# Counting edges in 39 steps, one of them 17 destinations wide, in a two-layer graph kernel

## The chip, the cores and the metric

The kernel runs on one core of a Trainium2 chip. The metric is device time in microseconds (us) of one execution. The kernel before takes 991.92 us, the median of 3 runs (991.07 to 992.71).

## The reference, cut to what matters

There are 625 nodes with 1024 features and 20000 edges (source, destination, one of 8 types), sorted by destination. A graph attention layer comes first, a relational layer with a gate second; each adds its input and is normalized over the features.

```python
def _L0_gnn_ref(x, W, a, src, dst):
    h = x @ W
    al = h @ a_l
    ar = h @ a_r
    e = jnp.exp(-jax.nn.leaky_relu(al[src] + ar[dst], negative_slope=NEG_SLOPE))
    rowsum = jax.ops.segment_sum(e, src, num_segments=N)
    h_prime = jax.ops.segment_sum(e[:, None] * h[dst], src, num_segments=N)
    h_prime = h_prime / (rowsum[:, None] + EPS)
    return jax.nn.elu(h_prime)

    # second layer
    for r in range(weight.shape[0]):
        mask = (edge_type == r).astype(x.dtype)
        sums = jax.ops.segment_sum(msgs * mask[:, None], dst, num_segments=n)
        cnt = jax.ops.segment_sum(mask, dst, num_segments=n)
        mean = sums / jnp.maximum(cnt, 1.0)[:, None]
        out = out + mean @ weight[r]
```

Both layers need the edges only as counts: how many edges of type r go from source s to destination d. The first layer multiplies these counts, summed over r, into its attention matrix; the second multiplies each type's counts with x.

## The kernel before

The five engines run programs written out by hand, tied by semaphores. Four stages follow each other on TensorE: h = x @ W in two halves of 512 columns (0 to 51 us); counting the edges, with the rest of that product, the sums of counts and the first attention products between the counting steps (51 to 148 us); the end of the attention, ELU, normalization and transposes (148 to about 190 us); and the second layer, a long row of fp32 products in three parts each (high by high, low by high, high by low).

Counting works as follows. The edges lie in 158 tiles of 128, one edge per partition. For each edge, `oh_s` holds a one-hot of its source within a block of 128 nodes (128 columns). VectorE builds a second one-hot for a *step* w (a window of `WIN` = 16 destinations): 640 columns, one for each pair of (source block, type) code and destination in the window, 40 codes by 16 destinations. That is `table` plus 16w compared with the edge's `key` (L968). TensorE multiplies the transposed first by the second in two matmuls of 320 columns into two banks of the accumulation memory (L1341). Both engines take tiles in *passes* of `BODY` = 5 tiles. The number of passes of a step depends on the data: setup code turns the smallest and largest destination of each tile and the edges of each step's window (`win_edge`) into a first tile and a number of passes, and each engine loads them from `lohi_row` at the head of the step (L345). A step counts ceil(tiles / 5) passes.

There are 40 steps for 640 destinations, though there are 625 nodes: the fortieth serves destination 624 alone. A step is, on TensorE: two small matmuls that clear the banks (L1356, waiting until ScalarE has copied the last step that used them), the passes, a small matmul that closes (L1359). On ScalarE: `copy_window`, one copy of 128x640 from the banks to `Cst` (L595). On VectorE: five one-hots for each pass.

Two buffers hold the one-hots, `hot` for even steps and a part of `w_raw` for odd ones, five slots each; semaphores `built` and `counted` guard each slot. So VectorE builds the next step's while TensorE multiplies this step's, but two passes of one step share one buffer. From step 12 on the steps alternate between two pairs of banks, 2/3 and 5/6 (`window_bank`, which counts from the last step back); before that all use 5/6.

The other work of this stage is tied to step numbers. After step 8(j+1) and the three behind it, TensorE sums a block of 128 destinations over the types (L1293) and turns it (L1300). `att_mult(3)` (VectorE, L948) and `att_high(3)` (ScalarE, L627) come after step 38, `att_low(3)` (VectorE, L953) after step 39. Behind the last step TensorE starts `att_h(1, 0, ...)` (L1306 to L1308) into banks 2 and 3, waiting for the copies of all steps but the last, then L1293 for the last block, waiting for the copies of all.

Of the kernel before, what the change touches and what calls it, by code (L numbers as in the profile page):

```python
# [5 lines left out]
def gat_rgcn_kernel(nc, dst_cols, src_cols, type_cols, dst_units, xT, x, weights, a, bias, b_gate, counts_dram, out):  # L6
# [4 lines left out]
    i32 = mybir.dt.int32  # L11
# [24 lines left out]
    WIN = P // R  # L36
    WINDOWS = NP // WIN
    PER = P // WIN
    CODES = NT * R
    SPLIT = NP // 2  # L40
    NE = N + N % 2
    NCOL = [(0, 320), (320, NE - 320)]
# [6 lines left out]
    GB = 3  # L49
    SUMS = 2 * KT  # L50

    def rows(t):
# [6 lines left out]
    with ctx:  # L59
# [33 lines left out]
        key = sb("key", [P, ALL_TILES], f32)  # L93
        table = sb("table", [P, NP], f16)
        ident = ident_r[:, :].bitcast(f32)
# [3 lines left out]
        with ExitStack() as first:  # L99
            xT_raw = sb("xT_raw", [P, KT, N], f32, first)  # L100
            iota_i = sb("iota_i", [P, NP], i32, first)
            h_raw = sb("h_raw", [P, NT, H2], f32, first)
# [56 lines left out]

        hots_in = [hot[:, :], w_ring[:, :, :].rearrange("p b n -> p (b n)").bitcast(bf16)[:, 0:BODY * NP]]  # L160

        def one_hot(w, s, c0=0, c=NP):
            return hots_in[w % 2][:, s * NP + c0:s * NP + c0 + c]

        edge_rows = table[0:2, :].bitcast(f32)

# [185 lines left out]
        def _(sp):  # L352
# [13 lines left out]
            def flush(j):  # L366
                sp.wait_ge(window_copied, PER * (j + 1) + 1)
                for m in range(NT):
                    sp.dma_start(C_dram[:, m, :, j * P:(j + 1) * P].rearrange("r p n -> p r n"),
                                 Cst[j % 2][:, m, :, :].bitcast(f32)).then_inc(flushed[j], 16)  # L370
# [95 lines left out]
        def _(pool):  # L466
            pool.iota(iota_i[:, :], pattern=[[1, CODES], [P // 2, WIN]], base=0, channel_multiplier=0).then_inc(pool_consts, 1)
            pool.iota(part_col[:, :], pattern=[[0, 1]], base=0, channel_multiplier=1,
# [76 lines left out]
        def _(act):  # L545
# [43 lines left out]
            def copy_window(w):  # L589
                j, v = divmod(w, PER)  # L590
                act.wait_ge(window_counted, w + 1)
                if v == 0 and j >= 2:
                    act.wait_ge(flushed[j - 2], 16 * NT)
                    act.wait_ge(turned, 2 * (j - 1))
                nc.scalar.copy(Cst[j % 2][:, :, :, v * WIN:(v + 1) * WIN].rearrange("p m r d -> p (m r) d")  # L595
                               .rearrange("p (b q) d -> p b q d", b=2),
                               ps[:, window_bank(w) * H2:(window_bank(w) + 2) * H2]
                               .rearrange("p (b n) -> p b n", b=2)[:, :, 0:SPLIT]
                               .rearrange("p b (q d) -> p b q d", d=WIN)).then_inc(window_copied, 1)
# [205 lines left out]
        def _(dve):  # L805
# [21 lines left out]
            step(v.memset(dots[:, :], 0.0))  # L827
            dve.wait_ge(pool_consts, 6)
            v.tensor_scalar(table[:, :], iota_i[:, :], 1.0 / (P // 2), None, ALU.mult)
            v.tensor_scalar(ident_r[:, :], iota_s[:, :], part_col[:, :], None, ALU.is_equal)  # L830
            v.tensor_scalar(win_edge[:, 0:1], part_col[:, :], float(WIN), None, ALU.mult)
            step(v.tensor_scalar(win_edge[:, 1:2], part_col[:, :], float(WIN), float(WIN - 1), ALU.mult, ALU.add))
            def split_low(n, k):
# [128 lines left out]
            def hots(w):  # L962
                turn = turns[w % 2]
                n = dve.snap(turn, min_val=1, max_val=WINDOWS * ALL_TILES)
                tile = dve.snap(tile_at, min_val=0, max_val=ALL_TILES - BODY)
                for s in range(BODY):
                    dve.wait_ge(counted[w % 2][s], n)
                    v.tensor_scalar(one_hot(w, s), table[:, :], float(WIN * w),  # L968
                                    key[:, ds(tile + s, 1)], ALU.add, ALU.is_equal).then_inc(built[w % 2][s], 1)
                dve.reg_add(turn, turn, 1)  # L970
                dve.reg_add(tile_at, tile_at, BODY)
# [244 lines left out]
        def _(pe):  # L1216
# [69 lines left out]
            def sum_counts(j, part):  # L1286
                m0, m1 = turn_blocks(part)
                pe.wait_ge(window_copied, PER * (j + 1) + 1)
                if turn_bank(j, part) == 4:
                    pe.wait_ge(turned_read, 2 * j + part)  # L1290
                o = bank(turn_bank(j, part), c=(m1 - m0) * P).rearrange("p (m n) -> p m n", n=P)
                for r in range(R):
                    last = mm(o, ident_r[:, :], Cst[j % 2][:, m0:m1, r, :], start=r == 0, stop=r == R - 1)  # L1293
                last.then_inc(summed, 1)
# [39 lines left out]
            def counts(w):  # L1334
# [3 lines left out]
                for s in range(BODY):  # L1338
                    pe.wait_ge(built[w % 2][s], n)
                    for c in range(2):  # L1340
                        last = mm(bank(window_bank(w) + c, c=SPLIT), oh_s[:, ds(edge + s * P, P)],  # L1341
                                  one_hot(w, s, c * SPLIT, SPLIT),
                                  start=False, stop=False, skip_group_check=True)
# [248 lines left out]
```

## Time and profile before

| | |
|---|---|
| median of 3 runs | 991.92 us (991.07 to 992.71) |
| the profiled execution | 990.91 us, its span 989.1 us |
| TensorE matmul busy | 977.2 us, 99% |
| VectorE, ScalarE, GpSimd busy | 392.9, 281.7, 254.2 us |
| mean granted TensorE clock | 0.998 |
| one-hots built (L968) | 210, 381 ns each |
| counting matmuls (L1341) | 420, 299 ns each, 210 on each buffer |

The profile shows one execution. The span is the time between its first and last instruction. Matmuls overlap one another, so the time that one costs is the distance of starts, not its duration. Idle time of an engine costs something only where TensorE, which is busy all along, waits for it.

### The profile page before, as it was taken

The numbers are of one execution on the slowest core, as the hardware profiler recorded it, in microseconds if no ns is written. First come the engines' busy times: TensorE is split into PE (matmuls) and PEld (weight loads), VectorE is DVE, ScalarE is ACT, GpSimd is POOL, SyncE is SP. The second block draws the span as 40 slices with busy tenths as digits, with TensorE's granted clock in tenths as the row PEclk, the third lists the DMA queues.
The fourth block names the chain that finished last, engine by engine and source line by source line (L and its number), as shares of the span: only waits on it lengthen the run. The fifth ranks groups of instructions, "written<-read, shape, count | busy, mean of one in ns | idle before, by whom it ended". The sixth has DMA issues, their size and how long they took to land.

```text
span 989.1 us, 14598 instructions
## 1 busy us (share of the span) xinstructions
PE 977.2 (99%) x5138; PEld 820.9 (83%) x5138; DVE 392.9 (40%) x749; ACT 281.7 (28%) x486; POOL 254.2 (26%) x196
## 2 busy tenths in 40 slices
PE   9999999999999999999999999999999999999997
PEld 7866778778898888888888988988988988888886
DVE  7998883712222331430530430331232232202277
ACT  4324554741122122121221221222222212212432
POOL 0000002084322323213223122142141231326730
PEclk9999999999999999999999999999999999999999
DMA  7204657067210411411411321231141051212402
GB/s 266 64 2 129 186 182 228 11 227 201 77 42 22 163 44 32 151 43 43 140 53 43 116 77 43 95 99 42 30 153 41 12 172 36 71 52 66 139 1 104
DMA packets 69005, 91.41 MB, mean 92 GB/s; under 512 B 9396, under 2 KB 35475, under 8 KB 68838
## 3 DMA queue, kind: packets, MB, share of 16 engines
q1 hardware_dynamic: 68818, 90.57, 29.1%
q8 instruction: 23, 0.38, 0.2%
q10 hardware_dynamic: 148, 0.32, 0.1%
q14 instruction: 16, 0.13, 0.0%
HBM read 75.19 MB, written 15.69 MB: 92 GB/s over the span
## 4 chain that ended last, share of the span: by engine, by line
PE 96%; DVE 2%; ACT 1%; issue 1%; POOL 0%; DVEq 0%; ACTq 0%
PE ps L1225 21%; PE ps L1227 21%; PE ps L1226 21%; PE ps L1493 9%; PE ps L1492 9%; PE ps L1341 6%; PE ps L1293 1%; PE ps L1548 1%; PE ps L1547 1%; PE ps L1546 1%; PE ps L1306 1%; PE ps L1307 1%; PE ps L1308 1%; PE ps L1481 0%; PE ps L1513 0%
## 5 line engine op out<-in xcount | busy, mean ns | idle before, releaser
L481 POOL TENSOR_TENSOR w_lo<-w_raw,w_hi 128x512 fp32r<-128x512 f32 x168 | 217.4, 1299 | 693.4 <-ACT w_hi L557 693.2
L557 ACT CAST w_hi<-w_raw 128x512 fp32r<-128x512 f32 x183 | 114.0, 625 | 463.8 <-PE ps L1227 397.6
L1225 PE MATMUL ps<-w_hi,M_hi 128*128 128x512 f32 (+1 forms) x550 | 215.6, 392 | 0.1
L1227 PE MATMUL ps<-w_lo,M_hi 128*128 128x512 f32 (+1 forms) x550 | 214.3, 390 | 0.0
L1226 PE MATMUL ps<-w_hi,M_lo 128*128 128x512 f32 (+1 forms) x550 | 214.2, 389 | 0.0
L1090 DVE SCALAR_TENSOR_TENSOR u<-ps,scale,u 128x512 f32<-128x512 f32 (+1 forms) x90 | 66.4, 745 | 315.0 <-PE ps L1227 315.0
L1492 PE MATMUL ps<-C_hi,x_hi 128*128 128x320 f32 (+3 forms) x640 | 184.5, 306 | 0.0
L1493 PE MATMUL ps<-C_hi,x_lo 128*128 128x320 f32 (+3 forms) x640 | 184.3, 306 | 0.0
L1225 PE MATMUL ps<-w_hi,M 128*128 128x512 f32 (+1 forms) x360 | 140.3, 390 | 0.0
L1227 PE MATMUL ps<-w_lo,M 128*128 128x512 f32 (+1 forms) x360 | 140.2, 390 | 0.0
L1226 PE MATMUL ps<-w_hi,M 128*128 128x512 f32 (+1 forms) x360 | 140.2, 389 | 0.0
L1492 PEld LDWEIGHTS ps<-C_hi,x_hi 128*128 128x128 f32 (+1 forms) x640 | 120.7, 189 | 0.9
L1225 PEld LDWEIGHTS ps<-w_hi,M_hi 128*128 128x128 f32 (+1 forms) x550 | 101.9, 185 | 23.3 <-issue 0.6
L1493 PEld LDWEIGHTS ps<-C_hi,x_lo 128*128 128x128 f32 (+1 forms) x640 | 120.9, 189 | 0.3
L1227 PEld LDWEIGHTS ps<-w_lo,M_hi 128*128 128x128 f32 (+1 forms) x550 | 101.8, 185 | 23.1
L1226 PEld LDWEIGHTS ps<-w_hi,M_lo 128*128 128x128 f32 (+1 forms) x550 | 101.9, 185 | 22.2
L1227 PEld LDWEIGHTS ps<-w_lo,M 128*128 128x128 f32 (+1 forms) x360 | 66.7, 185 | 15.0
L1226 PEld LDWEIGHTS ps<-w_hi,M 128*128 128x128 f32 (+1 forms) x360 | 66.7, 185 | 14.7
L1225 PEld LDWEIGHTS ps<-w_hi,M 128*128 128x128 f32 (+1 forms) x360 | 66.7, 185 | 14.6
L1095 DVE TENSOR_REDUCE col_sum<-C_hi 128x640 f32<-128x3200 f32 x8 | 47.9, 5987 | 42.8 <-DMA C_hi<-C_dram 42.8
L1111 DVE TENSOR_TENSOR M_lo<-ps,M_hi 128x320 fp32r<-128x320 f32 x64 | 31.0, 484 | 53.3 <-ACT M_hi L729 53.3
L1111 DVE TENSOR_TENSOR M<-ps,M 128x320 fp32r<-128x320 f32 x64 | 31.0, 484 | 53.3 <-ACT M L729 53.3
(189 smaller groups left out, 829.2 us busy)
## 6 DMA issues: line engine op xcount, KB each, us to landing
w_raw<-weights SPq DMA_DIRECT2D x184, 256.0 KB, 2.9
C_dram<-Cst SPq DMA_DIRECT2D x25, 512.0 KB, 6.1
C_hi<-C_dram SPq DMA_DIRECT2D x8, 1600.0 KB, 7.0
z<-b_gate SPq DMA_DIRECT2D x5, 512.0 KB, 9.6
u<-bias SPq DMA_DIRECT2D x5, 512.0 KB, 7.8
xT_raw<-xT SPq DMA_DIRECT2D x7, 312.5 KB, 6.7
u<-x SPq DMA_DIRECT2D x4, 512.0 KB, 4.8
last_raw<-weights SPq DMA_DIRECT2D x8, 256.0 KB, 5.5
```

Of the source, the lines that this page charges most:

```text
L481: pool.tensor_tensor(w_lo[k % RING][:, :], w_raw[k % RING][:, :], w_hi[k % RING][:, :].bitcast(f32), ALU.subtract).then_inc(w_lo_done, 1)
L557: nc.scalar.copy(w_hi[k % RING][:, :], w_raw[k % RING][:, :]).then_inc(w_hi_done, 1)
L1090: v.scalar_tensor_tensor(u[r, t, half * H2:(half + 1) * H2], bank(t, rows(t)), scale[odd][r, t:t + 1], u[r, t, half * H2:(half + 1) * H2], ...
L1095: v.tensor_reduce(col_sum[:, :], C_hi[:, :, :].bitcast(f32).rearrange("p m n -> p n m"), X, ALU.add)\
L1111: v.tensor_tensor(M_lo[1 - odd][:, e // 2, c0:c0 + cn], bank(5 + (e + 1) % GB, c=cn), M_hi[1 - odd][:, e // 2, c0:c0 + cn].bitcast(f32), A ...
L1225: mm(o, lhs_hi[:, k, c], w_hi[k % RING][:, :], start=opens, stop=False)
L1226: mm(o, lhs_lo[:, k, c], w_hi[k % RING][:, :], start=False, stop=False)
L1227: last = mm(o, lhs_hi[:, k, c], w_lo[k % RING][:, :], start=False, stop=closes_)
L1293: last = mm(o, ident_r[:, :], Cst[j % 2][:, m0:m1, r, :], start=r == 0, stop=r == R - 1)
L1341: last = mm(bank(window_bank(w) + c, c=SPLIT), oh_s[:, ds(edge + s * P, P)], one_hot(w, s, c * SPLIT, SPLIT), start=False, stop=False, ski ...
L1492: mm(o, x1_hi[r, m, f], C_hi[r, m, c0:c0 + cn], start=m == 0, stop=False)
L1493: last = mm(o, x1_lo[r, m, f], C_hi[r, m, c0:c0 + cn], start=False, stop=m == NT - 1)
```

## The change

There are 39 steps. Step 37 (`WIDE`) takes 17 destinations, 592 to 608, and step 38 takes 609 to 624; `win_at(w)` gives a step's first destination. The wide step's one-hots have `HOT` = 680 columns, and its second matmul 360. Its `copy_window` has an ACT copy of 128x40 ahead of the usual one, for the seventeenth destination. `win_edge` is built with two more VectorE instructions and `table` is 40 columns longer, for which there is one more iota on GpSimd. Since `window_bank` counts back from the last step, the bank pairs of all steps from 12 on change places: step 12 is now on 5/6 and 13 is the first on 2/3. The hunks that are left out replace `PER * (j + 1) + 1` by its minimum with 40 in two waits (`flush`, `sum_counts`).

```diff
-    WINDOWS = NP // WIN
+    WINDOWS = N // WIN
+    WIDE = WINDOWS - 2
     PER = P // WIN
     CODES = NT * R
     SPLIT = NP // 2
+    HOT = NP + CODES
+    assert N == WINDOWS * WIN + 1 and WIDE % 2 == 1
...
+    def win_at(w):
+        return WIN * w + (w > WIDE)
+
+    def cols(w):
+        return HOT if w == WIDE else NP
...
-            pool.iota(iota_i[:, :], pattern=[[1, CODES], [P // 2, WIN]], base=0, channel_multiplier=0).then_inc(pool_consts, 1)
+            pool.iota(iota_i[:, 0:NP], pattern=[[1, CODES], [P // 2, WIN]], base=0, channel_multiplier=0).then_inc(pool_consts, 1)
+            pool.iota(iota_i[:, NP:HOT], pattern=[[1, CODES]], base=WIN * (P // 2), channel_multiplier=0).then_inc(pool_consts, 1)
...
+                d0 = win_at(w) - j * P
+                if w == WIDE:
+                    nc.scalar.copy(Cst[j % 2][:, :, :, d0 + WIN].rearrange("p m r -> p (m r)"),
+                                   bank(window_bank(w) + 1, c0=SPLIT, c=CODES))
+                nc.scalar.copy(Cst[j % 2][:, :, :, d0:d0 + WIN].rearrange("p m r d -> p (m r) d")
...
-            v.tensor_scalar(win_edge[:, 0:1], part_col[:, :], float(WIN), None, ALU.mult)
-            step(v.tensor_scalar(win_edge[:, 1:2], part_col[:, :], float(WIN), float(WIN - 1), ALU.mult, ALU.add))
+            v.tensor_scalar(win_edge[:, 0:1], part_col[:, :], float(WIDE), None, ALU.is_gt)
+            step(v.tensor_scalar(win_edge[:, 1:2], part_col[:, :], float(WIDE), float(WIN - 1), ALU.is_ge, ALU.add))
+            for c in range(2):
+                step(v.scalar_tensor_tensor(win_edge[:, c:c + 1], part_col[:, :], float(WIN), win_edge[:, c:c + 1], ALU.mult, ALU.add))
...
-                    v.tensor_scalar(one_hot(w, s), table[:, :], float(WIN * w),
+                    v.tensor_scalar(one_hot(w, s, c=cols(w)), table[:, 0:cols(w)], float(win_at(w)),
                                     key[:, ds(tile + s, 1)], ALU.add, ALU.is_equal).then_inc(built[w % 2][s], 1)
...
-                        last = mm(bank(window_bank(w) + c, c=SPLIT), oh_s[:, ds(edge + s * P, P)],
-                                  one_hot(w, s, c * SPLIT, SPLIT),
+                        n_c = SPLIT if c == 0 else cols(w) - SPLIT
+                        last = mm(bank(window_bank(w) + c, c=n_c), oh_s[:, ds(edge + s * P, P)],
+                                  one_hot(w, s, c * SPLIT, n_c),
                                   start=False, stop=False, skip_group_check=True)
```

TensorE's program of the last three steps before (37, 38 and 39; `ISA` rows are waits and register work, `built1_0` is slot 0 of the odd steps' buffer, the branch closes the loop over passes; the repeated slots are left out):

```order
L1341 ISA [waits built1_0]
L1341 MATMUL ps<-w_raw,oh_s 128x320 x2
...
L1357 COMPARE_AND_BRANCH
L1359 MATMUL ps<-zeros 128x2
...
L1341 ISA [waits built0_0]
L1341 MATMUL ps<-hot,oh_s 128x320 x2
...
L1341 ISA [waits built1_0]
L1341 MATMUL ps<-w_raw,oh_s 128x320 x2
...
L1306 MATMUL ps<-M,M_hi 128x512 [waits window_copied]
```

And of the last two steps in the changed kernel (37, the wide one, and 38; its L1323 is the L1306 of before, its L1377 the L1359):

```order
L1359 ISA [waits built1_0]
L1359 MATMUL ps<-w_raw,oh_s 128x320
L1359 MATMUL ps<-w_raw,oh_s 128x360
...
L1375 COMPARE_AND_BRANCH
L1377 MATMUL ps<-zeros 128x2
...
L1359 ISA [waits built0_0]
L1359 MATMUL ps<-hot,oh_s 128x320 x2
...
L1323 MATMUL ps<-M,M_hi 128x512 [waits window_copied]
```

The last step's code is gone, and the attention products stand behind an even step. The program doesn't say how often a loop runs.

VectorE's program behind the one-hots of step 38, before:

```order
L968 TENSOR_SCALAR hot<-table,key 128x640
...
L948 SCALAR_TENSOR_TENSOR tmp<-tmp,att 128x640 [waits turned_read,exp_done]
L345 TENSOR_LOAD lohi_row
...
L968 TENSOR_SCALAR w_raw<-table,key 128x640
...
L953 TENSOR_TENSOR M_lo<-tmp,M_hi 128x640 [waits attT_hi_done]
L948 SCALAR_TENSOR_TENSOR tmp<-tmp,att 128x640 [waits turned_read,exp_done]
```

And in the changed kernel:

```order
L985 TENSOR_SCALAR w_raw<-table,key 128x680
...
L985 TENSOR_SCALAR hot<-table,key 128x640
...
L965 SCALAR_TENSOR_TENSOR tmp<-tmp,att 128x640 [waits turned_read,exp_done]
L970 TENSOR_TENSOR M_lo<-tmp,M_hi 128x640 [waits attT_hi_done]
L965 SCALAR_TENSOR_TENSOR tmp<-tmp,att 128x640 [waits turned_read,exp_done]
```

`att_mult(3)` no longer has a step's one-hots between itself and `att_low(3)`, which waits for ScalarE; no one-hot stands behind either.

## Rows read from the trace of the kernel before

**Rows 1.** The page, part 4: shares of the chain that ended last, by engine.
```profile
PE 96%; DVE 2%; ACT 1%; issue 1%; POOL 0%; DVEq 0%; ACTq 0%
```
**Rows 2.** Groups by form: one-hots and counting matmuls; count, busy us, mean ns, idle before.
```profile
L968 DVE TENSOR_SCALAR w_raw<-table,key 128x640 bf16<-128x640 f16 x105 | 32.9, 381 | 4.3 <-issue 2.2 <-PE ps L1341 1.7 <-DVE w_lo L835 0.3
L968 DVE TENSOR_SCALAR hot<-table,key 128x640 bf16<-128x640 f16 x105 | 32.9, 382 | 4.5 <-issue 4.1 <-PE ps L1341 0.4
L1341 PE MATMUL ps<-w_raw,oh_s 128*128 128x320 bf16 x210 | 31.9, 299 | 1.0 <-DVE w_raw L968 0.7
```
**Rows 3.** Timeline of TensorE at steps 37 to 39: start us, duration us.
```profile
143.44 1.53 PE L1341 MATMUL ps<-w_raw,oh_s 128*128 128x320 bf16 x10
144.81 0.17 PE L1359 MATMUL ps<-zeros 128*128 128x2 bf16 x1
...
145.10 1.53 PE L1341 MATMUL ps<-hot,oh_s 128*128 128x320 bf16 x10
146.47 0.17 PE L1359 MATMUL ps<-zeros 128*128 128x2 bf16 x1
...
146.88 1.53 PE L1341 MATMUL ps<-w_raw,oh_s 128*128 128x320 bf16 x10
...
148.27 0.48 PE L1306 MATMUL ps<-M,M_hi 128*128 128x512 f32 x1
...
149.72 2.52 PE L1293 MATMUL ps<-Cst,ident 128*128 128x384 f32 x16
```
**Rows 4.** Windows of these steps: length, busy us (instructions) of each engine, clock.
```profile
143.37:148.27 4.90, 4.71 (x41) 3.33 (x40) 3.46 (x11) 2.70 (x4) 0.00 (x0) 1.00 0.94 337
```
**Rows 5.** Timeline of TensorE at steps 10 and 11.
```profile
81.43 2.94 PE L1341 MATMUL ps<-hot,oh_s 128*128 128x320 bf16 x20
84.20 0.17 PE L1359 MATMUL ps<-zeros 128*128 128x2 bf16 x1
...
85.35 0.19 PE L1356 MATMUL ps<-zeros 128*128 128x2 bf16 x2
85.80 1.53 PE L1341 MATMUL ps<-w_raw,oh_s 128*128 128x320 bf16 x10 [0.26 <-DVE w_raw L968]
```
**Rows 6.** Timeline of TensorE between steps 12 and 13.
```profile
89.98 0.17 PE L1359 MATMUL ps<-zeros 128*128 128x2 bf16 x1
...
90.06 1.52 PE L1341 MATMUL ps<-w_raw,oh_s 128*128 128x320 bf16 x10
```
**Rows 7.** Timeline of VectorE at steps 37 to 39.
```profile
140.85 1.57 DVE L968 TENSOR_SCALAR w_raw<-table,key 128x640 bf16<-128x640 f16 x5 [1.09 <-PE ps L1341]
142.83 1.57 DVE L968 TENSOR_SCALAR hot<-table,key 128x640 bf16<-128x640 f16 x5 [0.41 <-PE ps L1341]
144.31 0.82 DVE L948 SCALAR_TENSOR_TENSOR tmp<-tmp,att 128x640 f32<-128x640 f32 x1
145.05 1.57 DVE L968 TENSOR_SCALAR w_raw<-table,key 128x640 bf16<-128x640 f16 x5
```
**Rows 8.** Timeline of ScalarE, the copy of step 39.
```profile
148.48 0.69 ACT L595 CAST Cst<-ps 128x640 fp32r<-128x640 f32 x1 [0.45 <-PE ps L1359]
```
**Rows 9.** Timeline, all engines, between steps 11 and 12.
```profile
87.40 0.69 ACT L595 CAST Cst<-ps 128x640 fp32r<-128x640 f32 x1 [1.56 <-PE ps L1359]
...
88.57 0.19 PE L1356 MATMUL ps<-zeros 128*128 128x2 bf16 x2
```
**Rows 10.** Timeline of GpSimd and VectorE at the start.
```profile
0.84 0.79 POOL L467 IOTA iota_i<- 128x640 int32 x1 [0.39 <-POOLq L1586]
...
2.37 0.16 POOL L476 IOTA iota_body<- 128x32 f32 x1
...
2.65 0.49 DVE L829 TENSOR_SCALAR table<-iota_i 128x640 f16<-128x640 int32 x1 [0.84 <-POOL iota_body L476]
...
3.32 0.14 DVE L832 TENSOR_SCALAR win_edge<-part_col 128x1 f32<-128x1 f32 x1
...
4.46 0.43 DVE L886 CAST w_hi<-w_raw 128x512 fp32r<-128x512 f32 x1 [1.00 <-DMA w_raw<-weights]
```

More of the change, by code:

```diff
@@ L93, in gat_rgcn_kernel @@
         key = sb("key", [P, ALL_TILES], f32)
-        table = sb("table", [P, NP], f16)
+        table = sb("table", [P, HOT], f16)
         ident = ident_r[:, :].bitcast(f32)
@@ L100, in gat_rgcn_kernel @@
             xT_raw = sb("xT_raw", [P, KT, N], f32, first)
-            iota_i = sb("iota_i", [P, NP], i32, first)
+            iota_i = sb("iota_i", [P, HOT], i32, first)
             h_raw = sb("h_raw", [P, NT, H2], f32, first)
@@ L158, in gat_rgcn_kernel @@
             x1_hi = sb("x1_hi", [P, NT, D], f32r, late)
-        hots_in = [hot[:, :], w_ring[:, :, :].rearrange("p b n -> p (b n)").bitcast(bf16)[:, 0:BODY * NP]]
+        hots_in = [hot[:, :], w_ring[:, :, :].rearrange("p b n -> p (b n)").bitcast(bf16)[:, 0:BODY * HOT]]
         def one_hot(w, s, c0=0, c=NP):
-            return hots_in[w % 2][:, s * NP + c0:s * NP + c0 + c]
-        edge_rows = table[0:2, :].bitcast(f32)
+            at = s * (NP, HOT)[w % 2] + c0
+            return hots_in[w % 2][:, at:at + c]
+        edge_rows = table[0:2, 0:NP].bitcast(f32)
         g_parts = [m[:, :, :].rearrange("p a b -> p (a b)") for m in (M_hi[0], M_lo[0])]
@@ L366, in flush @@
             def flush(j):
-                sp.wait_ge(window_copied, PER * (j + 1) + 1)
+                sp.wait_ge(window_copied, min(PER * (j + 1), WINDOWS) + 1)
                 for m in range(NT):
@@ L594, in copy_window @@
                     act.wait_ge(turned, 2 * (j - 1))
-                nc.scalar.copy(Cst[j % 2][:, :, :, v * WIN:(v + 1) * WIN].rearrange("p m r d -> p (m r) d")
+                d0 = win_at(w) - j * P
[3 more added lines that the diff above has]
+                nc.scalar.copy(Cst[j % 2][:, :, :, d0:d0 + WIN].rearrange("p m r d -> p (m r) d")
                                .rearrange("p (b q) d -> p b q d", b=2),
@@ L827, in _ @@
             step(v.memset(dots[:, :], 0.0))
-            dve.wait_ge(pool_consts, 6)
+            dve.wait_ge(pool_consts, 7)
             v.tensor_scalar(table[:, :], iota_i[:, :], 1.0 / (P // 2), None, ALU.mult)
             v.tensor_scalar(ident_r[:, :], iota_s[:, :], part_col[:, :], None, ALU.is_equal)
-            v.tensor_scalar(win_edge[:, 0:1], part_col[:, :], float(WIN), None, ALU.mult)
-            step(v.tensor_scalar(win_edge[:, 1:2], part_col[:, :], float(WIN), float(WIN - 1), ALU.mult, ALU.add))
+            v.tensor_scalar(win_edge[:, 0:1], part_col[:, :], float(WIDE), None, ALU.is_gt)
+            step(v.tensor_scalar(win_edge[:, 1:2], part_col[:, :], float(WIDE), float(WIN - 1), ALU.is_ge, ALU.add))
+            for c in range(2):
+                step(v.scalar_tensor_tensor(win_edge[:, c:c + 1], part_col[:, :], float(WIN), win_edge[:, c:c + 1], ALU.mult, ALU.add))
             def split_low(n, k):
@@ L1287, in sum_counts @@
                 m0, m1 = turn_blocks(part)
-                pe.wait_ge(window_copied, PER * (j + 1) + 1)
+                pe.wait_ge(window_copied, min(PER * (j + 1), WINDOWS) + 1)
                 if turn_bank(j, part) == 4:
```

## The prediction, on record before the changed kernel ran

> **What bounds the kernel now.** I read the chain that ended last first. It lies on TensorE for 96% [rows 1], so a change is worth what it takes from or adds to TensorE's program, and what another engine does counts only from the point where TensorE waits for it. Next come the groups by form. In the counting stage VectorE builds 105 one-hots in each buffer, 210 in all [rows 2], which is 42 passes of five for 40 steps: two steps take two passes. One of them is step 10, where the timeline shows 20 matmuls in one step [rows 5]. Over the whole stage TensorE waited 0.7 us for one-hots of the odd buffer [rows 2]. VectorE is close behind, though. Third is the timeline of the last three steps. On TensorE, step 37 begins at 143.44, step 38 at 145.10, step 39 at 146.88, and the attention products at 148.27 us [rows 3], at the full granted clock, with 4.71 of 4.90 us counted as busy [rows 4]. The change is decided in these 4.83 us (148.27 - 143.44). Behind them no instruction of TensorE changes, and a shift is carried to the end.
>
> Ten matmuls of a pass take 1.37 us of TensorE (143.44 to 144.81, 145.10 to 146.47) [rows 3]. From there to the next step's first counting matmul pass 0.29 and 0.41 us [rows 3]: the closing and clearing matmuls and the sequencer's work at the head of a step. Elsewhere that takes 0.08 us (89.98 to 90.06) [rows 6]. So one plain step costs 1.37 + 0.08 to 0.41 us, or 1.45 to 1.78 us, and that is the most that a step less could save.
>
> **Does the pass go?** This is the step of the argument on which the size hangs, and it is decided by the data. I took the destinations from the reference's inputs. 18917 edges have a destination under 592, 19448 one under 608, 19471 one under 609, and 19965 one under 624. In tiles of 128, step 37 before (592 to 607) lies in tiles 147 to 151, five tiles and one pass. The wide step (592 to 608) has 554 edges, from place 147.79 to 152.12 in tiles, so tiles 147 to 152: six, and two passes. Step 38 (609 to 624) has tiles 152 to 156, five, one pass. The same arithmetic on all 40 steps of before gives two passes for steps 1 and 10 alone, 42 in all, as rows 2 count, and step 10 is the one that rows 5 show with 20 matmuls; so I trust it. After the change there are again 42 passes. The fortieth step goes, but its pass comes back in step 37.
>
> **The sum on TensorE.** The wide step: two passes in one loop. At step 10, 20 matmuls took 84.20 - 81.43 = 2.77 us [rows 5], against 2 x 1.37 = 2.74 us for two single passes, so the way back in the loop costs 0.03 us. To this come ten matmuls with 40 more columns each. A matmul of 320 columns takes 0.137 us, so 0.43 ns a column, 0.017 us a matmul and 0.17 us for ten. The bounds are nothing (if a matmul were held by its weight load) and twice that. Then one head of a step, between 0.08 and 0.45 us (0.29, 0.41, and 85.80 - 85.35 = 0.45 [rows 3, 5, 6]); I take 0.35, the mean of the two at this very place. Then step 38 with 1.37 us, and 0.03 us to the attention products (146.88 + 1.37 = 148.25, against 148.27, so 0.02). In all 2.77 + 0.17 + 0.35 + 1.37 + 0.02 = 4.68 us, against 4.83 us before: 0.15 us less. With the bounds: 0.6 us less (head 0.08, no cost of columns) to 0.1 us more (head 0.45, twice the cost of columns).
>
> The trace puts 0.43 ns on a column when 320 are divided by their distance of starts. The Trainium skill ("TensorE: Matmul & The Clock Gate", section "Back-to-back issue gap") speaks against such a division for streams of weight load and matmul: it gives about 81 ns for 128 columns and 131 ns for 512, that is 0.13 ns a column. By it the ten matmuls would add 0.05 us and not 0.17, and the kernel would gain 0.27 us; but it would also put a matmul of 320 columns near 0.106 us, and the row shows 0.137, so the sum goes by the row.
>
> **What lies beside.** *VectorE's one-hots.* Ten of the wide step have 680 columns in place of 640. One of 640 takes 381 ns [rows 2] and a VectorE instruction of one column 0.14 us [rows 10]; the slope is (381 - 140) / 639 = 0.38 ns, so 40 columns add 15 ns, between 0 and 24 (381 x 40 / 640). Starts lie (1.57 - 0.38) / 4 = 0.30 us apart [rows 7], so 0.315 in the wide step. *Pass 2 of the wide step* shares its buffer with pass 1, so its slot 0 waits until TensorE has counted slot 0 of pass 1: that starts at 143.44 and its second matmul ends about 0.14 + 0.30 us later [rows 2, 3], at 143.88. With 0.1 for the semaphore VectorE starts at 144.0 and has slot s at 144.4 + 0.315 s. TensorE wants slot s at 143.44 + 1.37 + 0.08 + 0.03 + 0.29 s = 144.9 + 0.29 s. Slot 4 is there at 145.65 and wanted at 146.1: covered by 0.4 us. *Step 38's one-hots.* VectorE ends pass 2 at 145.65. Between two steps it stood 0.41 us [rows 7], which covers the head of the next. It starts at 146.05 and has slot s at 146.45 + 0.30 s. TensorE wants them from 143.44 + 2.94 + 0.35 = 146.73, 0.274 apart. Slot 0 is covered by 0.3 us, slot 4 by 0.15. This is the thinnest cover in the change. *`att_mult(3)`* stood ahead of step 39's one-hots (144.31 [rows 7]). It now stands behind step 38's, at 147.55, and `att_low(3)` behind it; with one ScalarE copy between them they end near 150.6, while TensorE has 16 sums at 149.72 for 2.4 us and attention products of earlier blocks to do first [rows 3]. Covered.
>
> *ScalarE's second copy* (128x40) has no row. It costs between nothing and the 0.69 us of 128x640 [rows 8]. The first attention products write banks 2 and 3, which the wide step now uses, and wait for its copy. The step closes at 146.4; with 0.24 us to ScalarE's start (148.48 against 148.25 [rows 3, 8]) and 0.69 + 0.69 the copy is done at 148.0 at worst, and TensorE is there at 148.1. It is covered at either bound. The copy of step 38 is done about 0.95 us behind its close, and the sums that need it stand 1.45 us behind (148.27 to 149.72) [rows 3]. Covered too.
>
> *The bank pairs* change places. Only step 12 gets a new wait: it now uses the banks of step 11. That copy ends at 88.09 and step 12 clears at 88.57 [rows 9], since other products lie between them. Covered by 0.48 us. Step 13 loses such a wait and was never late for it. From step 14 on each step waits for the copy two steps back, as before.
>
> *The start.* GpSimd has one more iota, of 40 columns: near the 0.16 us of 32 [rows 10], at most the 0.79 of 640. The table's 40 columns add 0.03 us, and the two new VectorE instructions 0.14 us each with a wait of about 0.05 us: in all 0.16 + 0.03 + 0.38 = 0.57 us. VectorE stood 1.00 us there, waiting for the first weights [rows 10]. So nothing, and at the upper bound (0.79 + 0.41 = 1.2) 0.2 us. The window of the limits has 39 rows in place of 40, which changes no length.
>
> The sum is 0.15 us off the profiled execution, 990.91 to 990.76 us (its span 989.1 to 988.95; the 1.8 us around it stay). The median of the runs is 1.0 us above the profiled execution, so I forecast 991.8 us for it. A measurement of this kernel can tell about 0.2%, 2 us, from no change. The median's own runs lie 1.6 us apart.
>
> **Rivals.**
>
> *A. The pass goes with the step.* If the wide step counted in one pass, the gain would be a whole step less the columns of five tiles: 1.37 + 0.35 - 0.09 = 1.6 us, at most 1.78 + noise: 990.3 us. For it speaks that the step's code is gone. Against it speak the six tiles of the input. Even then it stays within 0.2%.
>
> *B. The shared buffer makes TensorE wait: slower than before.* The place is the wide step's second pass and step 38 behind it. Behind the double step 10, TensorE waited 0.26 us for VectorE at step 11, with a head of 0.45 us [rows 5]. There VectorE had other work as well, which it hasn't here. If VectorE is late at step 38 by more than the cover of 0.15 us, TensorE loses what is above that. As much as at step 11 (0.26), with the head at 0.45 and an uncovered 0.2 at the start, makes -0.15 + 0.26 + 0.10 + 0.2 = 0.4 us more: 992.3 us. It decides from a delay of VectorE of 0.3 us on; with 0.41 us between steps rather than 0.7 it doesn't come.
>
> *C. Something that no row shows moves everything by more than its terms,* as the place of code or of a transfer might in the second layer, where the loops of each relation repeat a shift 8 times: a quarter us each makes 2 us, 989.8 or 993.8. Nothing in the profile speaks for it, since the loops' instructions are the same.
>
> **How the numbers follow.** Forecast (a gain of 0.15 us, within 0.6 less and 0.1 more) 0.77; A 0.04; B 0.12; C 0.07, to either side. A and B both lie within 0.2%, and C beyond it, with a little from the spread of medians: faster by over 0.2% 0.05, within 0.2% 0.91, slower 0.04. The terms alone give 991.3 to 992.3. With the runs' spread of about 0.8 to either side, and A and most of C inside, the range is 990.0 to 993.3 us.
>
> **What would show it.** In the changed kernel: still 210 one-hots, ten of them of 680 columns; ten counting matmuls of 360 columns, with starts about 17 ns further apart; step 37 with 20 matmuls in about 2.94 us; from its first matmul to the first attention product 4.7 us. VectorE waits for TensorE within step 37 and TensorE for nobody in step 38. The copy of 128x40 takes 0.2 to 0.4 us, and the first attention product doesn't wait for ScalarE. VectorE still waits for the first weights at the start. Only five one-hots of 680 columns, and 205 in all, would make A right and my counting of tiles wrong; a wait of TensorE for `hot` at step 38 would make B right; a difference of over 1 us with all this in place would be C, and would have to be found behind 180 us.

## The result: 0.85% slower, and the profile after

| | before | after |
|---|---|---|
| median | 991.67 us (4 runs, 991.07 to 992.71) | 1000.21 us (4 runs, 999.14 to 1000.54) |
| ratio to before, 95% | | 1.0085 (1.0073 to 1.0097) |
| the profiled execution, its span | 990.91, 989.1 us | 1000.08, 998.3 us |
| mean granted TensorE clock | 0.998 | 0.998 |

The forecast was 991.8 us, with a range up to 993.3. The kernel is 8.5 us slower. The chain that ended last reads in the kernel after as in the kernel before [rows 1]. Its shares are whole per cents, so this only hints that the loss isn't a wait:

```profile
PE 96%; DVE 2%; ACT 1%; issue 1%; POOL 0%; DVEq 0%; ACTq 0%
```

I looked first where the change is. The groups by form of the kernel after (count, busy us, mean ns, idle before) answer to [rows 2]: 210 one-hots as before, ten of them wide, and ten wide matmuls.

```profile
L985 DVE TENSOR_SCALAR hot<-table,key 128x640 bf16<-128x640 f16 x105 | 32.8, 381 | 4.7 <-issue 4.7
...
L985 DVE TENSOR_SCALAR w_raw<-table,key 128x640 bf16<-128x640 f16 x95 | 29.9, 382 | 3.7 <-issue 2.6 <-PE ps L1359 0.6 <-DVE w_lo L852 0.3
...
L985 DVE TENSOR_SCALAR w_raw<-table,key 128x680 bf16<-128x680 f16 x10 | 3.2, 394 | 2.1 <-PE ps L1359 2.1
L1359 PE MATMUL ps<-w_raw,oh_s 128*128 128x360 bf16 x10 | 2.9, 316 | 0.0
```

The timeline of TensorE in the kernel after, steps 37 and 38 (start us, duration us), answers to [rows 3]. It joins matmuls of one tile into one row and prints the form of the first, so the `x20` holds the ten wide ones:

```profile
144.56 3.05 PE L1359 MATMUL ps<-w_raw,oh_s 128*128 128x320 bf16 x20
147.45 0.17 PE L1377 MATMUL ps<-zeros 128*128 128x2 bf16 x1
147.82 0.19 PE L1374 MATMUL ps<-zeros 128*128 128x2 bf16 x2 [0.21 <-issue]
148.13 1.53 PE L1359 MATMUL ps<-hot,oh_s 128*128 128x320 bf16 x10
149.50 0.17 PE L1377 MATMUL ps<-zeros 128*128 128x2 bf16 x1
149.53 0.47 PE L1323 MATMUL ps<-M,M_hi 128*128 128x512 f32 x1
```

From step 37 to the attention products is 149.53 - 144.56 = 4.97 us, 0.14 more than before and not 0.15 less. That isn't 9.2 us, the difference of the spans (998.3 - 989.1). Step 37 began 1.12 us later than before (144.56 against 143.44), so 9.2 - 1.12 - 0.14 = 7.9 us arise behind 149.53, where I had written that no instruction changes. There the windows of the kernel after (length, busy us and instructions of PE, PEld, DVE, ACT, POOL, clock) show a TensorE that is busy all along, at the full granted clock:

```profile
300.00:500.00 200.00, 200.00 (x1023) 171.84 (x1022) 59.53 (x79) 42.35 (x81) 52.44 (x42) 1.00 0.25 79
500.00:700.00 200.00, 200.00 (x1023) 171.44 (x1022) 52.60 (x76) 41.72 (x80) 52.75 (x41) 1.00 0.22 69
```

The same windows of the kernel before hold more matmuls in the same 200 us:

```profile
300.00:500.00 200.00, 200.00 (x1033) 173.34 (x1032) 59.50 (x79) 43.11 (x82) 52.66 (x42) 1.00 0.25 80
500.00:700.00 200.00, 200.00 (x1033) 173.22 (x1032) 53.33 (x77) 42.50 (x81) 53.74 (x42) 1.00 0.22 68
```

So TensorE got through 1% fewer matmuls, without a wait. The groups by form say which got longer. Of the kernel after:

```profile
L1242 PE MATMUL ps<-w_hi,M_hi 128*128 128x512 f32 x440 | 172.8, 393 | 0.1
...
L1242 PE MATMUL ps<-w_hi,M 128*128 128x512 f32 x288 | 114.6, 398 | 0.0
L1243 PE MATMUL ps<-w_hi,M 128*128 128x512 f32 x288 | 114.3, 397 | 0.0
L1244 PE MATMUL ps<-w_lo,M 128*128 128x512 f32 x288 | 113.6, 394 | 0.0
...
L1565 PE MATMUL ps<-M_hi,M 128*128 128x512 f32 x32 | 12.7, 397 | 0.0
```

And of the kernel before:

```profile
L1225 PE MATMUL ps<-w_hi,M_hi 128*128 128x512 f32 x440 | 172.7, 393 | 0.1
...
L1225 PE MATMUL ps<-w_hi,M 128*128 128x512 f32 x288 | 112.2, 390 | 0.0
L1227 PE MATMUL ps<-w_lo,M 128*128 128x512 f32 x288 | 112.2, 390 | 0.0
L1226 PE MATMUL ps<-w_hi,M 128*128 128x512 f32 x288 | 112.2, 390 | 0.0
...
L1546 PE MATMUL ps<-M_hi,M 128*128 128x512 f32 x32 | 12.4, 389 | 0.0
```

Products with `M_hi0` kept their time. Those with `M`, which is the second tile (`M1`: the matrices of odd relations, `h_parts` in the attention, an operand of the last products), went from 390 ns to between 394 and 398 ns. The six groups of `w` by `M` grew by 7.2 us of busy time (420.6 to 427.8, with those of the last block of 113 nodes), the last products by 0.9 and the attention's by 0.3: 8.4 us. Matmuls overlap, so I also added up the distances of starts in the two traces: they grew by 7.2, 0.8 and 0.1 us, 8.1 us in all, near the 7.9 of the timeline.

What of `M1` did the diff change? Its place. The hunk that does it isn't among those shown ahead, where I wrote that only two waits are left out:

```diff
-        table = sb("table", [P, NP], f16)
+        table = sb("table", [P, HOT], f16)
```

`table` got 80 bytes longer in each partition. In the built program, where tiles lie one behind another in the order of the code and in units of 32 bytes, it grew by 96, and everything allocated behind it moved by 96 bytes: `M1` from byte 85888 to 85984 of each partition. `M_hi0` (16512), `w_hi` and `w_lo` (from 65664, their buffers 2048 apart) lie ahead of `table` and stayed.

### The profile page after: what moved, and what is told of

It reads as the page before. It is cut to its first block, busy times and chain, and to the rows that moved or that the text cites. A ratio compares the mean times of both kernels' runs of the same rounds, so it can differ in the third digit from the quotient of the medians.

```text
span 998.3 us, 14588 instructions
## 1 busy us (share of the span) xinstructions
PE 986.7 (99%) x5135; PEld 821.9 (82%) x5135; DVE 393.7 (39%) x751; ACT 280.2 (28%) x486; POOL 254.7 (26%) x197
## 4 chain that ended last, share of the span: by engine, by line
PE 96%; DVE 2%; ACT 1%; issue 1%; POOL 0%; DVEq 0%; ACTq 0%
PE ps L1242 21%; PE ps L1243 21%; PE ps L1244 21%; PE ps L1511 9%; PE ps L1510 9%; PE ps L1359 6%; PE ps L1310 1%; PE ps L1565 1%; PE ps L1564 1%; PE ps L1566 1%; PE ps L1323 1%; PE ps L1325 1%; PE ps L1324 1%; PE ps L1499 0%; PE ps L1531 0%
## 5 line engine op out<-in xcount | busy, mean ns | idle before, releaser
L1242 PE MATMUL ps<-w_hi,M 128*128 128x512 f32 (+1 forms) x360 | 142.9, 397 | 0.0
L1243 PE MATMUL ps<-w_hi,M 128*128 128x512 f32 (+1 forms) x360 | 142.6, 396 | 0.0
L1244 PE MATMUL ps<-w_lo,M 128*128 128x512 f32 (+1 forms) x360 | 142.2, 395 | 0.0
```

The source lines that it names most:

```text
L1242: mm(o, lhs_hi[:, k, c], w_hi[k % RING][:, :], start=opens, stop=False)
L1243: mm(o, lhs_lo[:, k, c], w_hi[k % RING][:, :], start=False, stop=False)
L1244: last = mm(o, lhs_hi[:, k, c], w_lo[k % RING][:, :], start=False, stop=closes_)
```

## The experiments

All ratios are to the kernel before, run on the same chip, with 95% intervals. A name with b_ is an edit of the kernel before, one with a_ an edit of the kernel after. In the products with `w` a tile `M` (`M_hi0`, `M_lo0` or `M1`) gives the weights, and `w` (`w_hi` or `w_lo`) is the moving tile, which streams past them. "Distance" is the first byte of the weights' tile less that of the moving tile, in bytes of a partition, modulo 256. It was 0 in the kernel before for `M1` and `w`, and for `M_hi0` and `w`.

### Is it the place? Padding alone, and the change without the shift

b_shift32, b_shift64 and b_shift96 are the kernel before with a tile that nobody uses, 8, 16 or 24 floats long:

```diff
         table = sb("table", [P, NP], f16)
+        pad = sb("pad", [P, 24], f32)
```

a_m1_first is the whole change, with `table` allocated behind `M1`, which so lies at 84608; what is behind `table` keeps its shift of 96 bytes.

```diff
-        table = sb("table", [P, HOT], f16)
...
         M1 = sb("M1", [P, 2, KT, NP], f32r)
+        table = sb("table", [P, HOT], f16)
```

> The kernel before, with 96 unused bytes per partition behind table and nothing else: all tiles behind it lie where the changed kernel has them (M1 at byte 85984 in place of 85888). Theory P (place: matmuls whose weights come from M1 take about 7 ns longer there; 1080 of them in the relations' loop and 144 behind it): 999 to 1000 us, and the mean of the matmuls on M (w_hi, M) near 397 ns in place of 390. Theory S (the 39 steps' program itself does it, by its code or its timing): no change, 991.7 us and 390 ns. Theory C (the slower first five matmuls, 0.8 us, are a matter of the single execution): whatever they show here, they make up at most 0.8 us.

Measured: 999.77 us, ratio 1.0077 (1.006 to 1.0093), products with `M` 398, 397 and 394 ns as in the kernel after.

> The kernel before with 64 unused bytes behind table. Theory P64 (what counts is a start at a multiple of 64 bytes): 991 to 992 us, as before, 390 ns. Theory P128 (a multiple of 128 bytes is wanted, or any move of M1 against the weights' buffers costs): 999 to 1000 us, 397 ns.

Measured: 998.46 us, 1.0062 (1.0045 to 1.0078). That lies in neither expected range: a start at a multiple of 64 bytes isn't enough, and the price is below that of 96 bytes.

> The kernel before with 32 unused bytes behind table. P64 and P128: 999 to 1000 us, as with 96. A theory by which only the upper part of a 128-byte line is bad (96 but not 32): 991 to 992 us.

Measured: 997.91 us, 1.0059 (1.0042 to 1.0076), again in neither range, but slow. So 32, 64 and 96 bytes each cost, and not the same.

> The changed kernel with the line of table moved behind that of M1: M1 now starts at byte 84608, a multiple of 128; all tiles behind M1 lie as in the changed kernel. Theory P with M1 alone: 991.5 to 992.5 us (the forecast of the change itself, 0.15 us less than before, to 0.3 more), 390 ns. If the tiles behind M1 (counts, x1) matter as well: between 993 and 999. Theory S: 1000 us, unchanged.

Measured: 991.37 us, 0.9995 (0.9986 to 1.0005). Its groups by form show 390 ns again:

```profile
L1242 PE MATMUL ps<-w_hi,M 128*128 128x512 f32 x288 | 112.3, 390 | 0.0
L1244 PE MATMUL ps<-w_lo,M 128*128 128x512 f32 x288 | 112.1, 389 | 0.0
L1243 PE MATMUL ps<-w_hi,M 128*128 128x512 f32 x288 | 112.0, 389 | 0.0
```

A pad without the change costs what the change cost, and the change without the shift of `M1` costs nothing. That is the cause in terms of the code. It also acquits the 96 bytes by which the tiles behind `M1` still moved.

### `M1`'s own place, or its distance from `w`?

Two rules fit so far: `M1` must begin at a suitable byte of its own, or it must lie a suitable distance from the tile that streams past it. b_m1_key puts `M1` ahead of `key` and `table`, at 83968, a multiple of 2048, whose distance to `w` is 128. b_m1_64 has it at 84672, distance 64.

```diff
+        with ExitStack() as first:
...
+        M1 = sb("M1", [P, 2, KT, NP], f32r)
         key = sb("key", [P, ALL_TILES], f32)
         table = sb("table", [P, NP], f16)
```

(b_m1_64: `key`, a pad of 16 floats, the same block, `table`.)

b_m0_32 puts 32 bytes ahead of `M_hi` and 32 behind `M_lo`: `M_hi0` moves by 32, `w` and `M1` by 64, so the distance of `M1` and `w` stays 0 and that of `M_hi0` and `w` becomes 224 (32 short of 256). b_w_32 moves `w` by 32 and `M1` by 64, so the distances are 32 for `M1` and again 224 for `M_hi0`.

```diff
+        pad = sb("pad", [P, 8], f32)
         M_hi = [sb("M_hi0", [P, KT, NP], f32r)]
         M_lo = [sb("M_lo0", [P, KT, NP], f32r)]
+        pad2 = sb("pad2", [P, 8], f32)
```

```diff
+        pad = sb("pad", [P, 8], f32)
         w_hi = [sb(f"w_hi{b}", [P, H2], f32r) for b in range(RING)]
         w_lo = [sb(f"w_lo{b}", [P, H2], f32r) for b in range(RING)]
+        pad2 = sb("pad2", [P, 8], f32)
```

> The kernel before with M1 and the tiles in its place moved ahead of key and table: M1 starts at byte 83968, a multiple of 2048, where before it was 85888 (a multiple of 128, not of 256). All tiles behind table keep their places. Theory P128 (a start at a multiple of 128 bytes is wanted, which of them doesn't matter): 991 to 992.5 us. Theory D (what counts is the distance between M1 and the weights' buffers, and 85888 and 84608 happened to be good): it may come out at 997 to 1000 us.

Measured: 997.52 us, 1.0061 (1.0044 to 1.0078). A round address of its own doesn't help `M1`.

> The kernel before with M1 ahead of table and 64 unused bytes ahead of M1: M1 at byte 84672, 64 bytes behind the place that was fast in the changed kernel with M1 first; the tiles behind it are shifted by 64. P128: 997.5 to 999 us, as with M1 at 85952. Theory N (the tiles behind M1 made the 6.5 us of the shift by 64, not M1): the same number, but with matmuls on M at 390 ns.

Measured: 998.06 us, 1.0065 (1.0048 to 1.0082), with products on `M` at 395 ns. At 390 ns the tiles behind `M1` would have been to blame (theory N), so they aren't.

> The kernel before with 32 unused bytes ahead of M_hi0 and 32 behind M_lo0: the first pair of M tiles starts off a multiple of 128 (16544), M1 at 85952, w_hi and w_lo shifted by 64. If the place of the weights' tile is what counts: the 1650 matmuls with weights from M_hi0 and M_lo0 go from 390 to 396 ns as well, 10 us, on the 6.5 us of M1: 1007 to 1010 us. If only M1 is touchy: 998 to 999 us. If the moving tile's place counts too (w_hi and w_lo at 64): more than 1010 us.

Measured: 1002.66 us, 1.0111 (1.0094 to 1.0128), in none of the three expected ranges.

> The kernel before with 32 unused bytes ahead of w_hi and 32 behind w_lo: the moving tiles of all products start at 65696, off a multiple of 128 by 32; M_hi0 and M_lo0 keep their places, M1 is at 85952. If only the weights' tile counts: 998 to 999 us and 390 ns for the matmuls with weights from M_hi0. If the moving tile counts as much: all 2730 matmuls of products are longer by 5 to 7 ns, 1008 to 1012 us.

Measured: 1008.52 us, 1.0169 (1.0152 to 1.0186), in the range for a moving tile that counts as much as the weights' tile.

What b_m0_32 shows of `M1` was expected by none of the theories, and that decides. Its groups by form:

```profile
L1227 PE MATMUL ps<-w_hi,M_hi 128*128 128x512 f32 x440 | 175.0, 398 | 0.1
L1228 PE MATMUL ps<-w_hi,M_lo 128*128 128x512 f32 x440 | 174.0, 395 | 0.0
L1229 PE MATMUL ps<-w_lo,M_hi 128*128 128x512 f32 x440 | 173.7, 395 | 0.0
L1227 PE MATMUL ps<-w_hi,M 128*128 128x512 f32 x288 | 112.3, 390 | 0.0
```

`M1` lies at byte 85952, where it also lies in b_shift64. The same group there:

```profile
L1226 PE MATMUL ps<-w_hi,M 128*128 128x512 f32 x288 | 113.7, 395 | 0.0
```

One address, 390 ns or 395: what differs is the distance to `w`. The reverse is there as well. b_m1_64 and b_shift64 have `M1` at two addresses, 1280 bytes apart, but at one distance, and the row of b_m1_64 is the same to the digit:

```profile
L1226 PE MATMUL ps<-w_hi,M 128*128 128x512 f32 x288 | 113.7, 395 | 0.0
```

Two more comparisons point the same way. `M_hi0` lies at 16544 in b_m0_32 and at 16512 in b_w_32, but at distance 224 in both, and its three products take 398, 395 and 395 ns in both. And in the last products the weights' tile is `M1`, but the moving tile is `M_hi0` or `M_lo0`. In b_m0_32 `M1` is at distance 0 from `w` and 32 from `M_hi0`, and the last products are slow (before: 389 ns, the L1546 above):

```profile
L1548 PE MATMUL ps<-M_hi,M 128*128 128x512 f32 x32 | 12.7, 396 | 0.0
```

The runs by distance (ns of the three products, high by high, high by low, low by high):

| kernel | `M1` at | distance `M1` to `w` | products with `M` | distance `M_hi0` to `w` | us |
|---|---|---|---|---|---|
| before | 85888 | 0 | 390, 390, 390 | 0 | 991.67 |
| a_m1_first | 84608 | 0 | 390, 389, 389 | 0 | 991.37 |
| b_m0_32 | 85952 | 0 | 390, 390, 390 | 224 | 1002.66 |
| b_shift32 | 85920 | 32 | 396, 396, 395 | 0 | 997.91 |
| b_w_32 | 85952 | 32 | 396, 396, 395 | 224 | 1008.52 |
| b_shift64 | 85952 | 64 | 395, 395, 394 | 0 | 998.46 |
| b_m1_64 | 84672 | 64 | 395, 395, 394 | 0 | 998.06 |
| b_shift96 | 85984 | 96 | 398, 397, 394 | 0 | 999.77 |
| after | 85984 | 96 | 398, 397, 394 | 0 | 1000.21 |
| b_m1_key | 83968 | 128 | 394, 394, 396 | 0 | 997.52 |

Each distance has its own durations. For 0, 32 and 64 the table has them at two or three places of the tiles; 96 and 128 were tried with `M1` at one place each. So it is the distance of the weights' tile from the moving tile that counts, and of those tried (0, 32, 64, 96, 128 and 224) only 0 is fast. b_w_32 leaves `w_raw`, into which the DMAs write, where it was, and the products with `M_hi0` are slow all the same, so its place isn't the cause. The price in b_m0_32 nearly adds up: the 1650 products with `M_hi0` and `M_lo0` grew by 9.4 us (644.1 to 653.5 us busy), the last products by 0.9 and the attention's by 0.5, 10.8 us against 11.2 us of the medians (991.51 to 1002.66).

### Does it reach the aggregation products?

The products of counts with x (L1492, L1493 of before) kept their time in the kernel after, though both tiles moved: `C_hi` and `x1_hi` moved together. b_x1_32 moves `x1_hi` alone by 32 bytes.

```diff
+            pad = sb("pad", [P, 8], f32, late)
             x1_hi = sb("x1_hi", [P, NT, D], f32r, late)
```

> The kernel before with 32 unused bytes ahead of x1_hi: its distance to C_hi, with which it is multiplied, changes from 81920 bytes (a multiple of 256) to 81952; x1_lo's stays. Theory D (a matmul is slower where its weights' tile and its moving tile are not a multiple of 256 bytes apart): the 640 matmuls of the aggregation with x1_hi are longer by some ns each, 1 to 5 us in all, 993 to 996.5 us, those with x1_lo unchanged or nearly. If this holds only for the products of 512 columns: 991.5 to 992 us.

Measured: 992.80 us, 1.0011 (1.0001 to 1.002). Its groups by form:

```profile
L1493 PE MATMUL ps<-C_hi,x_hi 128*128 128x320 f32 x256 | 76.7, 310 | 0.0
L1494 PE MATMUL ps<-C_hi,x_lo 128*128 128x320 f32 x256 | 76.3, 309 | 0.0
```

Before:

```profile
L1492 PE MATMUL ps<-C_hi,x_hi 128*128 128x320 f32 x256 | 75.8, 309 | 0.0
L1493 PE MATMUL ps<-C_hi,x_lo 128*128 128x320 f32 x256 | 75.7, 308 | 0.0
```

That is below the range of theory D (993 to 996.5 us) and above that of no effect (991.5 to 992). The distances of starts of all 1280 aggregation products add up to 185.3 us against 184.1 before: 1.2 us, or 1 ns each, not 7. And contrary to what was expected the products with `x1_lo`, whose distance didn't change, grew as well. The two kinds alternate, so while one with `x1_lo` streams, the weights of the next from `x1_hi` are loaded; that this is the reason is argued, not shown. These products have fewer columns and another order than those of the relations; which of these makes the price smaller wasn't tried.

### The change at its best: the wide step where five tiles are enough

The sum rested on six tiles in step 37, and rival A's price on five. a_w33_m1_first is a_m1_first with the wide step at 33 (destinations 528 to 544), which by the data has five tiles:

```diff
-    WIDE = WINDOWS - 2
+    WIDE = WINDOWS - 6
```

> The changed kernel with table moved behind M1, a second time and in five rounds, for the size of the change itself: by the prediction's sum 0.15 us less than before; by the first trace of it (step 37 to the attention products 4.96 us in place of 4.83) 0.1 us more. 991.2 to 992.2 us.

Measured: 991.06 us (11 runs), ratio 0.9996 (0.9987 to 1.0005).

> The same kernel with the wide step at 33 in place of 37 (17 destinations from 528, all later steps one up). By the input's edges step 33 then has five tiles and one pass, step 37 (593 to 608) one pass, so 41 passes and 205 one-hots in all. This is rival A made true: 1.4 to 1.8 us less than a_m1_first2, 989.5 to 990.5 us. If what a step less is worth is lost elsewhere (VectorE or ScalarE late), 991 to 992 us.

Measured: 989.32 us (11 runs, 988.88 to 989.74), ratio 0.9976 (0.9967 to 0.9985). That is 1.7 us below a_m1_first2, where rival A had 1.6. It beats both kernels. The groups by form have one pass less: 95 + 5 one-hots in this buffer.

```profile
L985 DVE TENSOR_SCALAR w_raw<-table,key 128x640 bf16<-128x640 f16 x95 | 29.8, 381 | 4.3 <-issue 2.7 <-PE ps L1359 1.2 <-DVE w_lo L852 0.3
L985 DVE TENSOR_SCALAR w_raw<-table,key 128x680 bf16<-128x680 f16 x5 | 1.7, 392 | 0.1
L1359 PE MATMUL ps<-w_raw,oh_s 128*128 128x360 bf16 x5 | 1.5, 315 | 0.0
```

The wide step, now 33, takes 136.16 - 134.72 = 1.44 us for its ten matmuls, against the 1.37 us of a plain pass:

```profile
134.72 1.60 PE L1359 MATMUL ps<-w_raw,oh_s 128*128 128x320 bf16 x10
136.16 0.17 PE L1377 MATMUL ps<-zeros 128*128 128x2 bf16 x1
```

From step 37 to the attention products it is 147.47 - 144.40 = 3.07 us, two plain steps:

```profile
144.40 1.53 PE L1359 MATMUL ps<-w_raw,oh_s 128*128 128x320 bf16 x10
...
146.07 1.53 PE L1359 MATMUL ps<-hot,oh_s 128*128 128x320 bf16 x10
...
147.47 0.48 PE L1323 MATMUL ps<-M,M_hi 128*128 128x512 f32 x1
```

## Why the prediction was wrong

**The step that failed** is the sentence "Behind them no instruction of TensorE changes, and a shift is carried to the end." The instructions are the same, and still 1176 of them (1080 of `w` by `M` and 96 of the last products) became 4 to 9 ns longer, and 120 in the attention by 1 to 3 ns on average; the timeline puts 7.9 us behind step 38. I had priced the 40 columns of `table` as 0.03 us of VectorE's time, and not as bytes that move every tile behind them. Rival C named the class (something that no row shows moves everything), but with the wrong places, code or a transfer, a chance of 0.07 and 2 us. An arithmetic was at hand that could have priced at least the exposure: some 3000 products of 512 columns, so a nanosecond on each is 3 us, more than the 2 us that can be measured.

**The pass** was right: six tiles, two passes, 210 one-hots. This was the step on which the size of the intended gain hung, and a_w33_m1_first confirms the price of the other case (A).

**The sum for steps 37 and 38** was 4.68 us and measured 4.97. The two terms were off in different directions:
- 20 matmuls took 147.45 - 144.56 = 2.89 us, forecast 2.94. The ten wide ones cost what was forecast: in the trace of the kernel after the next matmul starts 0.153 us behind a wide one and 0.136 us behind a plain one, so 17 ns for 40 columns, 0.17 us in all. In a_w33_m1_first the five wide ones make 0.07 us. What was too high is the base. At step 10 the eleventh matmul starts 0.176 us behind the tenth, which is the way back in the loop; in step 37 of the kernel after it starts 0.152 us behind it, no later than behind any other wide one.
- The head behind the double step took 148.13 - 147.45 = 0.68 us, forecast 0.35, upper bound 0.45. It is the mis-sized term, and alone puts these steps beyond the forecast's bound of 0.1 us more. The excess lies between the closing and the clearing matmul: 147.82 - 147.45 = 0.37 us, of which 0.21 are idle with the releaser "issue". Behind the single steps 37 and 38 of the kernel before it was 0.03 and 0.11 us (from 144.81 and 146.47 [rows 3]):

```profile
144.84 0.19 PE L1356 MATMUL ps<-zeros 128*128 128x2 bf16 x2
...
146.58 0.19 PE L1356 MATMUL ps<-zeros 128*128 128x2 bf16 x2
```

From the clearing to the first counting matmul it was 0.31 us, against 0.26 and 0.30 before. The clearing also waits for ScalarE's copy of step 36, but that was done at 145.28:

```profile
144.59 0.69 ACT L610 CAST Cst<-ps 128x640 fp32r<-128x640 f32 x1 [0.74 <-PE ps L1377]
```

a_m1_first shows the same head (0.67), so it isn't a matter of place. Behind the double steps 1 and 10 other products follow the closing matmul, so the profile before had no such row; I took the mean of heads behind single steps. Why the sequencer is late there wasn't isolated.

From the figures of the Trainium skill ("TensorE: Matmul & The Clock Gate", section "Back-to-back issue gap") for streams of weight load and matmul the estimate was 0.13 ns a column, 5 ns for 40 columns. The trace has 17 ns, so in this stream they don't hold, and going by the row was right.

**Rival B**, that VectorE makes TensorE wait, didn't come, though it had the right sign. The timeline of VectorE in the kernel after, beside [rows 7]:

```profile
142.09 1.62 DVE L985 TENSOR_SCALAR w_raw<-table,key 128x680 bf16<-128x680 f16 x5 [0.62 <-PE ps L1359]
145.16 1.63 DVE L985 TENSOR_SCALAR w_raw<-table,key 128x680 bf16<-128x680 f16 x5 [1.45 <-PE ps L1359]
147.21 1.57 DVE L985 TENSOR_SCALAR hot<-table,key 128x640 bf16<-128x640 f16 x5 [0.41 <-issue]
```

Pass 2 began 0.60 us behind TensorE's first matmul; I had 144.0 against 143.44, 0.56, with 0.1 us for the semaphore that no row showed. The 0.41 us between the steps is the figure that I used, and no matmul of step 38 has a wait in front of it. The wider one-hots took 394 ns, 13 more, against 15.

**What lies beside** held. The copy of 128x40 took 0.23 us, between its bounds, and nobody waited for it (timeline of ScalarE):

```profile
147.68 0.23 ACT L608 CAST Cst<-ps 128x40 fp32r<-128x40 f32 x1 [2.40 <-PE ps L1377]
```

At the start the iota took 0.16 us, and VectorE still waited for the first weights (timeline, against the 1.00 of [rows 10]); the two new instructions are in the first row:

```profile
3.63 0.35 DVE L849 SCALAR_TENSOR_TENSOR win_edge<-part_col,win_edge 128x1 f32<-128x1 f32 x2
...
4.51 0.43 DVE L903 CAST w_hi<-w_raw 128x512 fp32r<-128x512 f32 x1 [0.53 <-DMA w_raw<-weights]
```

**The 1.12 us ahead of step 37.** 0.78 us of it is there at step 0 already (52.01 against 51.23 us) and arises at the first products. Five of them take 2.33 us in the kernel after, behind seven matmuls on `ones_r`:

```profile
2.33 3.33 PE L1283 MATMUL ps<-ones_r 128*128 128x512 f32 x7 [2.33 <-issue]
5.45 2.33 PE L1272 MATMUL ps<-w_hi,M_hi 128*128 128x512 f32 x5
```

and 1.52 before:

```profile
5.45 1.52 PE L1255 MATMUL ps<-w_hi,M_hi 128*128 128x512 f32 x5
```

It is TensorE's clock. The trace's record of a granted clock of 1.00 begins at 5.79 us in the kernel before and at 7.54 us in the kernel after; the views print 1.00 ahead of it too, where there is no record. Until then matmuls of 512 columns mostly start 0.427 us apart, from then on about 0.227: by these distances the lower of its two levels, 1.2 GHz, and the upper, 2.4 GHz. The kernel after thus had five products at the lower level or across the change, the kernel before one. In a_m1_first, with the start of the kernel after, the record begins at 5.50 us (the five take 1.34 us) and in a_m1_first2, the same kernel again, at 5.52; in b_shift96, with the start of the kernel before, at 8.29 (2.37 us). So it doesn't go with the change. In b_x1_32, where every tile of this stage lies as in the kernel before, it begins at 6.66 (1.93 us), so it differs between executions without any change of place. Whether place adds something can't be told from these. The other 0.34 us is spread over steps 0 to 36 and wasn't traced.

Together: 0.78 + 0.34 + 0.14 + 7.94 = 9.2 us, the difference of the spans. Without the 0.78 us of the clock it is 8.4, near the 8.5 us of the medians.

## What to carry to other kernels

Where TensorE is the bound, a longer tile is also a change of every address behind it. Compare the bytes of all tiles in the two built programs before trusting that untouched code keeps its time, and put a tile that grows behind those that TensorE reads. If a whole row of products gets longer by a per cent or two without any wait, look at the distance between their two operands. Count the data before removing a step: moving the wide step by four places was worth 1.7 us, and removing a step whose pass comes back was worth nothing.

## What the runs showed of the hardware

- Matmuls of `w` by the full blocks of `M1` (fp32 operands, 512 columns) took 389 or 390 ns where the two tiles lie a multiple of 256 bytes apart in the partition, and 394 to 398 ns at 32, 64, 96 and 128 bytes; by distance of starts 227 ns and 232 to 235. Those with `M_hi0` and `M_lo0` took 393, 390 and 390 ns at 0 and 398, 395 and 395 at 224. With all products of `w` off it cost 1.7% of the kernel (b_w_32). In the cases tried the start of neither tile mattered by itself. The aggregation's products, of 320 and 306 columns, lost about 1 ns each in b_x1_32.
- The bf16 counting matmuls showed nothing of it. The odd buffer's distance to `oh_s` went from 0 in the kernel before to 160 in the kernel after, and its matmuls took 299 ns in both; `hot` is at 160 in all kernels, also with 299 ns. The comparison is weaker than above, since every second of these matmuls begins 640 bytes into its slot and so is off in any case.
- A wide counting matmul (360 columns in place of 320, bf16) cost 17 ns more by distance of starts, 0.153 against 0.136 us, in a row of such matmuls at the full granted clock.
- The Trainium skill ("TensorE: Matmul & The Clock Gate", section "Step-by-step: what each phase is for") says that loading the next weights doesn't take read bandwidth from the running matmul, and ("SBUF — State Buffer", section "🔬 SBUF: two separate sides") that TensorE's ports never wait for anyone. The table above is against reading this as "the place of the operands doesn't matter": 390 or 398 ns by distance alone. That the two reads of TensorE meet in some unit of memory would explain a rule of distances, but this is argued, not shown; nothing here separates it from other causes, such as the other engines' writes into the moving tiles.
